# A 4096 x 4096 layer of a feed-forward stack by seven products of quarters instead of eight, and the stack in three token passes instead of two

## The reference, cut to what matters

```python
xn = layernorm(x)                                  # x: 4 x 4096 x 1024
out = x + attention(xn) + ffn(xn)                  # 16 heads of 64, ALiBi bias
def ffn(x):                                        # weights are -1, 0, 1, each with a scale per output row
    h = silu(tlin(x, w1)) * tlin(x, w2)            # 1024 -> 4096
    h = gelu(tlin(h, h1))                          # 4096 -> 4096
    h = gelu(tlin(h, h2))                          # 4096 -> 4096
    return tlin(h, w3)                             # 4096 -> 1024
# tlin(x, w) = (x @ w.T) * s
```

## Time and profile before

| | |
|---|---|
| median of 3 runs | 3135.11 us (3134.59 to 3135.47) |
| profiled execution | 3135.08 us; span 3133.5 us on core 5 (the cores' spans: 3117.3 to 3133.5) |
| TensorE busy | 3071.9 us, 98% of the span, 14592 matmuls |
| VectorE / ScalarE / GpSimd busy | 557.1 / 920.4 / 150.5 us |
| the tail (L677) | 9216 matmuls, from 1127.3 us to the end |
| granted TensorE clock | 0.995 on core 5, 0.997 to 0.998 on the others |

### The profile page before, as it was taken

How to read it: one execution, slowest core, us unless ns; L and a number is a source line. 1 busy time by engine, 2 the same in 40 slices (tenths; PEclk the granted TensorE clock), 3 DMA queues, 4 the chain that set the end, 5 groups by cost and what they waited for, 6 DMA issues and landing times.

```text
span 3133.5 us, 37072 instructions; the slowest of 8 cores (3117.3 to 3133.5 us)
## 1 busy us (share of the span) xinstructions
PE 3071.9 (98%) x14592; PEld 1341.0 (43%) x14592; DVE 557.1 (18%) x871; ACT 920.4 (29%) x1420; POOL 150.5 (5%) x252
## 2 busy tenths in 40 slices
PE   5999999999999999999999999999999999999999
PEld 3543333333333344444444444444444444444444
DVE  4523454444545420000000000011000000000001
ACT  3538778777777710000000000000000000000000
POOL 1210000000000000000000000000000000000000
PEclk9999999999999999999999999999999999999999
DMA  7414332333334663443444444587444443443453
GB/s 169 122 28 80 61 70 68 63 66 65 69 80 90 142 160 71 81 78 71 81 74 75 81 75 74 123 201 164 76 81 74 75 81 71 77 81 72 76 105 117
DMA packets 80279, 279.32 MB, mean 89 GB/s; under 512 B 8304, under 2 KB 28912, under 8 KB 59632
## 3 DMA queue, kind: packets, MB, share of 16 engines
q0 software_dynamic: 36192, 192.95, 35.5%
q1 hardware_dynamic: 42768, 81.91, 8.2%
q10 hardware_dynamic: 1152, 2.10, 0.2%
HBM read 436.31 MB, written 33.55 MB: 150 GB/s over the span
## 4 chain that ended last, share of the span: by engine, by line
PE 91%; DMA 7%; DVE 1%; issue 0%; ACT 0%; SPq 0%; POOL 0%; DVEq 0%; ACTq 0%; POOLq 0%
PE PS L677 59%; PE PS L169 21%; PE PS L585 7%; PE PS L561 4%; DMA out<-UO 4%; DMA Wv<-Wv 1%; DMA xin<-xk 1%; DMA h_d<-HO 1%; PE PS L307 0%; DMA XO<-xT 0%; SPq L69 0%; DVE st L282 0%; DVE st L283 0%; DVE UO L706 0%; DVE xnb L296 0%
## 5 line engine op out<-in xcount | busy, mean ns | idle before, releaser
L677 PE MATMUL PS<-HBb,WB 128*128 128x512 bf16 x4608 | 998.0, 380 | 7.0 <-DVE UO L706 4.3
L677 PE MATMUL PS<-HBa,WB 128*128 128x512 bf16 x4608 | 995.0, 379 | 3.8 <-ACT HBa L691 2.7
L677 PEld LDWEIGHTS PS<-HBb,WB 128*128 128x128 bf16 x4608 | 451.3, 98 | 553.5 <-issue 12.1
L677 PEld LDWEIGHTS PS<-HBa,WB 128*128 128x128 bf16 x4608 | 450.7, 98 | 548.2 <-issue 5.2
L573 ACT ACTIVATE eT<-PS,p 128x512 bf16<-128x512 f32 x972 | 591.4, 691 | 93.6 <-PE PS L561 93.6
L169 PE MATMUL PS<-XN,W 128*128 128x512 bf16 x2048 | 565.0, 381 | 4.8 <-DVE HO L456 3.9
L706 DVE SCALAR_TENSOR_TENSOR UO<-PS,cv,UO 128x512 f32<-128x512 f32 x32 | 24.0, 751 | 1833.9 <-PE PS L677 1832.6
L691 ACT ACTIVATE HBa<-PS,cv 128x1024 bf16<-128x1024 f32 x64 | 71.3, 1114 | 933.6 <-PE PS L677 933.6
L691 ACT ACTIVATE HBb<-PS,cv 128x1024 bf16<-128x1024 f32 x64 | 71.3, 1114 | 799.9 <-PE PS L677 799.9
L169 PEld LDWEIGHTS PS<-XN,W 128*128 128x128 bf16 x2048 | 180.3, 98 | 280.1 <-issue 97.5
L585 PE MATMUL PS<-eT,V 128*128 128x512 bf16 x972 | 296.9, 380 | 0.0
(11 more groups left out here) (52 smaller groups left out, 750.8 us busy)
## 6 DMA issues: line engine op xcount, KB each, us to landing
WB<-h1sl POOLq DMA_DIRECT2D x64, 1024.0 KB, 8.9
WB<-h2sl POOLq DMA_DIRECT2D x64, 1024.0 KB, 8.8
W<-w POOLq DMA_DIRECT2D x64, 512.0 KB, 6.1
xin<-xk SPq DMA_DIRECT2D x32, 512.0 KB, 5.1
h_d<-HO SPq DMA_DIRECT2D x128, 128.0 KB, 5.2
WB<-w3sl POOLq DMA_DIRECT2D x16, 1024.0 KB, 9.1
HBa<-h_d SPq DMA_DIRECT2D x8, 1024.0 KB, 7.4
UO<-acc_d SPq DMA_DIRECT2D x32, 256.0 KB, 3.4
```

The source lines that it names most:

```text
L677: f = lambda e, o=o, W=W, c=c, n=n, src=src: e.matmul(o, W[:, c, :], src[:, c, n * 512:(n + 1) * 512], start=(c == 0), stop=(c == 31))
```

## The change

The tokens go in three passes of 684, 684 and 680 (`HN` is half a pass: 342, 342, 340). h1 and w3 are computed as before, with matmuls over `HN` tokens, two per weight tile. h2 is cut in quarters: output rows in halves (slab j is paired with slab j + 16), inputs in halves (the first and last 16 tiles of a slab), and tokens in halves. Each pair of slabs then gives four output tiles, rows by tokens, by Winograd's form of Strassen's scheme: seven products of 16 matmuls instead of eight.

- h1's Gelu is written in f32 (`G`); for each pair of its slabs DVE forms four differences and ACT casts five tiles, which gives the seven right-hand sides `h11, h21, h22, t1, t2, t3, t4` in bf16 (`A`).
- For each pair of h2's slabs DVE forms four weight sums s1 to s4 (integers from -4 to 4, exact in bf16), each in two pieces of 1024 columns, in eight buffers `BS`. `pieces` places them between the instructions of the products: five pieces of pair j + 1 in pair j, and three of pair j after its first product.
- The seven products go to seven banks in turn; ACT copies the first (`p1`), DVE joins them in seven operations (`comb`), and four Gelus on ACT write h2's output to `HQ`.
- Weight buffers: three that stay (`C0` to `C2`), with two more in h1 (`E0`, `E1`, inside `HQ`), one more in h2 (`F0`, inside `HP`) and two more in w3 (`G0`, `G1`, inside `A`). `uses` lists the loads in order; `feed` issues the next ones when their buffer is free and its stage's gate is open. In h2 both buffers of a pair come free together, after the pair's third product and its last piece.
- w3 waits for the last Gelu only ahead of its tiles 15 and 31, which come last. The loads of `UO` and `XO` and the stores of the result go through ACT; `load_h` stays on SP.
- A tile `HO` that crosses the edge of a pass is stored by two DMAs (64 stores more).

The core of the diff:

```diff
+HN = [342, 342, 340]
+TOK = [0, 684, 1368]
+A_SZ = 16 * 342 * 2
+P0_AT = 65792
+P1_AT = P0_AT + 4 * A_SZ
+C_AT = P1_AT + 4 * A_SZ
...
+    h_d = nc.dram_tensor("h_d", [3, 128, 32, 684], BF16, kind="Internal").ap()
+    acc_d = nc.dram_tensor("acc_d", [8, 128, QC], F32, kind="Internal").ap()
...
-    HB = [sb("HBa", [128, 32, 1024], BF16, 65536), sb("HBb", [128, 32, 1024], BF16, 0)]
-    WB = [sb(f"WB{i}", [128, 32, 128], BF16, 131072 + 8192 * i if i < 2 else Q_AT + 8192 * (i - 2))
-          for i in range(6)]
-    UO = [sb(f"UO{i}", [128, 512], F32, DYN_AT + 4096 * i) for i in range(3)]
-    XO = [sb(f"XO{i}", [128, 512], F32, DYN_AT + 4096 * i + 2048) for i in range(3)]
+    A = {k: sb("A" + k, [128, 16, 342], BF16, A_SZ * i if i < 6 else DYN_AT + 11008)
+         for i, k in enumerate(("h11", "h21", "h22", "t1", "t2", "t3", "t4"))}
+    HP = sb("HP", [128, 32, 684], BF16, P0_AT)
+    HQ = sb("HQ", [128, 32, 684], BF16, P1_AT)
+    SLOT = {n: sb("W" + n, [128, 32, 128], BF16, at) for n, at in (
+        ("C0", C_AT), ("C1", C_AT + 8192), ("C2", C_AT + 16384), ("E0", 131072), ("E1", 139264),
+        ("F0", P0_AT), ("G0", 0), ("G1", 8192))}
+    BS = [sb(f"BS{i}", [128, 16, 128], BF16, at) for i, at in enumerate(
+        [DYN_AT + 11008 + A_SZ, C_AT + 24576] + [P0_AT + 8192 + 4096 * i for i in range(6)])]
+    G = [[sb(f"G{k}{i}", [128, 2, 342], F32, DYN_AT + 2752 * (2 * k + i)) for i in range(2)] for k in range(2)]
+    TF = [[sb(f"TF{k}{i}", [128, 342], F32, P1_AT + 1376 * (2 * k + i)) for i in range(2)] for k in range(2)]
+    R = {k: sb("R" + k, [128, 342], F32, DYN_AT + 1376 * i)
+         for i, k in enumerate(("p1", "u2", "u3", "c11", "c12", "c21", "c22"))}
+    UO = [sb(f"UO{i}", [128, 2, 342], F32, 16384 + 5504 * i) for i in range(3)]
+    XO = [sb(f"XO{i}", [128, 2, 342], F32, 16384 + 5504 * i + 2752) for i in range(3)]
...
-                    SP.dma(l_ho[u % 3], h_d[T][:, hid, tl * 512:(tl + 1) * 512], ho[:, :])
+                    for p in range(3):
+                        a, b = max(tc * 512, TOK[p]), min(tc * 512 + 512, TOK[p] + 2 * HN[p])
+                        if a < b:
+                            SP.dma(l_ho[u % 3], h_d[p][:, hid, a - TOK[p]:b - TOK[p]],
+                                   ho[:, a - tc * 512:b - tc * 512])
...
-            POOL.dma(l_wb[s % 6], WB[s % 6][:, :, :], (h1sl, h2sl, w3sl)[stg][i])
-
-    def load_h(T, chunks, *toks):
+            load_use(0, (PE.sem, PE.n))
+            load_use(1)
...
+    uses, use_of = [], {}
+    c = ["C0", "C1", "C2"]
+    for p in range(3):
+        for stg, ring, n in ((0, c + ["E0", "E1"], 32), (1, [c[2], c[0], c[1], "F0"], 32),
+                             (2, [c[2], c[0], c[1], "G0", "G1"], 8)):
+            for k in range(n):
+                use_of[p, stg, k] = len(uses)
+                uses.append((p, stg, k // 2 + 16 * (k % 2) if stg < 2 else k, ring[k % len(ring)]))
+        c = [c[2], c[0], c[1]]
+    use_tok = {}
+    def load_use(u, *toks):
+        _, stg, i, slot = uses[u]
+        POOL.wait(*toks)
+        use_tok[u] = POOL.dma(l_s[slot], SLOT[slot][:, :, :], (h1sl, h2sl, w3sl)[stg][i])
+    def load_h(p, chunks, *toks):
         SP.wait(*toks)
-        SP.wait(*t_hstore[T])
+        SP.wait(*t_hstore[min(p, 1)])
         for c in chunks:
-            SP.dma(l_hb[c], HB[T][:, 4 * c:4 * c + 4, :], h_d[T][:, 4 * c:4 * c + 4, :])
+            SP.dma(l_hb[c], HP[:, 4 * c:4 * c + 4, 0:2 * HN[p]], h_d[p][:, 4 * c:4 * c + 4, 0:2 * HN[p]])
...
-                load_h(0, [0, 1], (PE.sem, PE.n))
-                for s in range(2):
-                    load_wb(s, (PE.sem, PE.n))
+                load_h(0, [0, 1, 2], (PE.sem, PE.n))
+                load_use(3, (PE.sem, PE.n))
+                load_use(4)
             if qc == 3 and P == 4:
-                load_h(0, [2, 7], (PE.sem, PE.n))
+                load_h(0, [3, 4], (PE.sem, PE.n))
...
+    slot_free = {n: () if n[0] != "E" and n[0] != "C" else None for n in SLOT}
+    gate = {("C", p): () for p in range(3)}
+    n_use = [5]
+    def feed():
+        while n_use[0] < len(uses):
+            p, _, _, slot = uses[n_use[0]]
+            if slot_free[slot] is None or (slot[0], p) not in gate:
+                break
+            load_use(n_use[0], *slot_free[slot], *gate[slot[0], p])
+            slot_free[slot] = None
+            n_use[0] += 1
+    def done(u, *toks):
+        slot_free[uses[u][3]] = toks
+        feed()
...
+        for j in range(16):
+            t_gl = []
+            for hf in range(2):
+                u = use_of[p, 0, 2 * j + hf]
+                W = SLOT[uses[u][3]]
+                pp = n_p[0] % 4
+                n_p[0] += 1
+                PE.wait(use_tok[u], bank_free[2 * pp], bank_free[2 * pp + 1])
+                for t in range(2):
+                    o = BK[2 * pp + t][:, 0:n]
+                    for c in range(32):
+                        if j == 0 and hf == 0 and t == 0 and c % 4 == 0:
+                            PE.wait(l_hb[c // 4].tok())
+                        f = lambda e, o=o, W=W, c=c, t=t, n=n: e.matmul(
+                            o, W[:, c, :], HP[:, c, t * n:(t + 1) * n], start=(c == 0), stop=(c == 31))
+                        if c == 31:
+                            tok = PE.do(f)
+                        else:
+                            PE.raw(f)
+                done(u, tok)
+                g = G[j % 2][hf]
+                ACT.wait(tok, *t_sum.get(j - 2, ()), *t_tmp)
+                c0 = 80 + j + 16 * hf
+                t_gl.append(ACT.do(lambda e, g=g, pp=pp, c0=c0, n=n: e.activation(
+                    g[:, :, 0:n], halves(pp, n), AF.Gelu, bias=0.0, scale=cv[:, c0:c0 + 1])))
+                bank_free[2 * pp] = bank_free[2 * pp + 1] = t_gl[-1]
...
+            DVE.wait(*t_gl, *t_last, *t_sum.get(j - 2, ()))
+            ACT.wait(*t_gl, *t_last)
+            d3 = diff(t3, h22, ALU.subtract, h12)
+            diff(to("t1"), h12, ALU.subtract, h11)
+            d2 = diff(t2, t3, ALU.add, h11, d3)
+            for k, a in (("h11", h11), ("h21", h21), ("h22", h22)):
+                cast(k, a, None)
+            cast("t3", t3, d3)
+            t_sum[j] = (diff(to("t4"), t2, ALU.subtract, h21, d2), cast("t2", t2, d2))
+        t_h1 = (PE.sem, PE.n)
+        gate["F", p] = (t_h1,)
+        feed()
...
+        def sums(j):
+            w11, w12, w21, w22 = quarters(j)
+            for k in range(4):
+                bsum[j, k + 1] = [n_s[0] % 8, None, None]
+                n_s[0] += 1
+            s1, s2, s3, s4 = [BS[bsum[j, k][0]] for k in (1, 2, 3, 4)]
+            for k, a, op, b, dst, dep in ((1, w21, ALU.add, w22, s1, None), (2, s1, ALU.subtract, w11, s2, 1),
+                                          (3, w11, ALU.subtract, w21, s3, None), (4, w12, ALU.subtract, s2, s4, 2)):
+                slot = bsum[j, k][0]
+                for h in range(2):
+                    DVE.wait(use_tok[use_of[p, 1, 2 * j]], use_tok[use_of[p, 1, 2 * j + 1]], *bs_free[slot])
+                    if slot >= 2:
+                        DVE.wait(t_h1)
+                    if dep:
+                        DVE.wait(bsum[j, dep][1 + h])
+                    r = slice(8 * h, 8 * h + 8)
+                    bsum[j, k][1 + h] = DVE.do(lambda e, dst=dst, a=a, b=b, op=op, r=r: e.tensor_tensor(
+                        dst[:, r, :], a[:, r, :], b[:, r, :], op))
+                    yield
...
+        def prod(k, a, j):
+            b = n_b[0] % 8
+            n_b[0] += 1
+            slot, t0, t1 = bsum[j, k]
+            PE.wait(bank_free[b], t0, t1)
+            tok = part(b, BS[slot], a, range(16), True, True)
+            bs_free[slot] = (tok,)
+            return b, tok
...
+        cur = sums(0)
+        pieces(cur, 5)
+        for j in range(16):
+            u1, u2 = use_of[p, 1, 2 * j], use_of[p, 1, 2 * j + 1]
+            w11, w12, w21, w22 = quarters(j)
+            b1, b2, b4 = [(n_b[0] + i) % 8 for i in range(3)]
+            n_b[0] += 3
+            PE.wait(use_tok[u1], bank_free[b1], bank_free[b2])
+            if j == 0:
+                PE.wait(*t_sum[14])
+                part(b1, w11, "h11", range(15), True, False)
+                part(b2, w12, "h21", range(15), True, False)
+                PE.wait(*t_sum[15])
+                m1 = part(b1, w11, "h11", [15], False, True)
+                m2 = part(b2, w12, "h21", [15], False, True)
+            else:
+                m1 = part(b1, w11, "h11", range(16), True, True)
+                m2 = part(b2, w12, "h21", range(16), True, True)
+            ACT.wait(m1, *fr["p1"])
+            p1 = bank_free[b1] = ACT.do(lambda e, n=n, b1=b1: e.copy(R["p1"][:, 0:n], BK[b1][:, 0:n]))
+            pieces(cur, 1)
+            PE.wait(use_tok[u2], bank_free[b4])
+            m4 = part(b4, w22, "t4", range(16), True, True)
+            pieces(cur, 1)
+            c11 = bank_free[b2] = comb("c11", "p1", b2, ALU.add, m2, p1)
+            gelu("c11", 0, 0, j, c11)
+            pieces(cur, 1)
```

(98 more changed lines are left out.)

102 lines of the change are left out of this document (46 added, 56 removed).

## The result

The changed kernel took 3118.85 us (median of 7 runs) beside 3135.93 us before; by ratio it stands at 0.9942 of before, 95% interval 0.9931 to 0.9954: 18 us gained, not 103, and outside the stated range.

What follows compares the result with a forecast made beforehand. TensorE was taken to bound the kernel, by number of matmuls times spacing. From 3135.08 us, -100.6 for matmuls, -2.7 for waits and +0.5 at the end made -102.8: 3032.3 us, range 3022 to 3072.

Steps and rivals of the forecast that it cites:

- The spacing at 342 columns: Tail matmuls: a line through three traced sizes gives 145.0 ns at 342 columns and 144.1 at 340.
- The sum on TensorE: h1, h2 and w3: 13056 matmuls make 1889.2 us against 1989.8 before, 100.6 less.
- VectorE in h2: DVE's pieces and joins in h2: 9.0 to 16.3 us a pair, hidden behind TensorE's 16.24; rival that DVE bounds h2, 0.07.
- Weights in h2: Slab loads in h2: 129 GB/s needed, DMA share 0.72, in time by 3 us for DVE and 10 for TensorE.
- The edges from h1 to h2: ACT's and DVE's work between h1 and h2 mostly hides behind matmuls; 1 us an edge, 3 in all.
- the mechanism I had named as a rival: Matmuls of 342 columns dearer because rows of 684 bytes start at new places; 7.9 ns each cancels the gain; chance 0.04.
- In the first two w3 stages: Edges at w3, where h chunks, two slabs and UO and XO tiles start together: 2 us each, between 0 and 10.
- The edges of w3 cost more: Rival: 10 us at each of two w3 edges and 4 at each from h1 to h2, +25, 3057 us; chance 0.07.
- It now goes by ACT's queue: At w3's edges, the result's store no longer waits behind h loads on SP's queue, which cost 4.3 us once before.
- The end: After the last matmul: a join over 680 columns for 512 and a 340 KB store for 256, together +0.5 us.
- Ahead of the tail: Before 1127 us only 64 extra stores are new, beside attention: 0 us, between -1 and +5.
- the 9.8 that the forecast allowed for waits and the clock: Tail: 3 us for h1-to-h2 edges, 4 for the first two w3 stages, 2.8 for the clock; 12.5 before.

Runs made afterwards that it cites:

- x4_prod8: Changed kernel with one of the seven products of each pair computed twice, so h2 has eight products again: 1.0307 of the kernel before, 3236 us.
- x10_axpool: Changed kernel with x added during attention (its loads on POOL), 344-element rows, eight UO buffers, banks emptied by ACT, w3's loads and stores on SP: 3064.7 and 3062.8 us.
- x3_pad344: Changed kernel with the rows of the seven right-hand sides 344 elements apart instead of 342: 0.9907 of the kernel before.
- x2_store_sp: Changed kernel with the stores of the result back on SP's queue, behind the eight loads of h: 0.9872 of the kernel before.
- x1_acc8: Changed kernel with eight UO and XO buffers instead of three, all loads issued at a w3 stage's start: 0.9887 of the kernel before.
- x5_h_late: Changed kernel with the eight loads of h issued two at a time after w3's second to fifth slab: 0.9940 of the kernel before.
- x6_evac: Changed kernel with 344-element rows, five buffers, w3's banks copied to SBUF by ACT, loads and stores on SP: 3104.1 and 3102.6 us.
- x7_no_h: Changed kernel without the second and third pass's h loads, DVE writing zeros instead (output wrong): 0.9780 of the kernel before, 3070 us.
- x8_fold: Changed kernel with x added during attention instead of in w3, so the XO loads leave the tail: 0.9871 of the kernel before.

## Why the prediction was wrong

Right, by its own steps:
- *The spacing at 342 columns*: 297.15 us for 2048 against 297.0. The Trainium skill ("TensorE: Matmul & The Clock Gate", "Back-to-back issue gap") has a sustained stream at about 81 ns for 128 columns and 131 for 512. These traces don't agree with either: 56 and 215.9 ns. The 11 ns more at 342 columns that the prediction held against itself came from the first of these alone.
- *The sum on TensorE*: x4_prod8 gives the removed product back for 115 us, and x10_axpool's core 1 has the whole tail at the forecast length.
- *VectorE in h2*: a piece of 1024 bf16 columns takes 685 ns, the lower end of the bounds; 512 columns in f32 took 687. The Trainium skill, "VectorE: DVE Perf Modes", section "The perf-mode tier table (the rule you actually need)", gives a bf16 tensor_tensor in SBUF twice the f32 rate, and the trace agrees. DVE is busy 133.7 of 263 us, 8.4 us a pair of slabs, less than the 9.0 to 16.3 allowed.
- *Weights in h2*: share 0.71 and 133 GB/s, forecast 0.72 and 129; no wait of TensorE for a slab. (That all eight cores had drawn more at once is not in the earlier trace rows, which show core 5 alone; in 2022 to 2125 us of the kernel before they moved 178 to 206 GB/s.)
- *The edges from h1 to h2*: no idle time; I had allowed 3 us.

Off in size: h2's matmuls took 146.9 ns instead of 145.0 because of the rows of 684 bytes, +9.0 us (x3_pad344). It is the mechanism I had named as a rival, at a quarter of the price it needed.

Failed: *"In the first two w3 stages ... I take 2 us for each, between 0 and 10."* They cost 35.0 and 31.5. So the step that failed is this term, 2 us where some 33 came, taken over from a reading of the kernel before in which a store behind the h loads was the cost. I had put the DMA rate of the earlier trace rows against h2's need, but never summed w3's. In its 74.2 us fall eight slabs (8.4 MB), h (5.6), the UO and XO tiles (5.6) and the stores (2.8): 22.4 MB, which would be 302 GB/s. The best average in the rows was 238, and 183 to 207 came [the windows above]. The rival "The edges of w3 cost more" named the right place, but took 10 us an edge, a third of what came.

Nor is one rate enough, since the queues differ. By the shares of the first edge shown above, 6.39 MB of weights took 38 us of all 16 engines (5.9 us a MB), h's 5.60 MB 17.8 us (3.2) and 3.50 MB of tiles and stores 12.8 us (3.7). As an estimate from these, the whole stage's bytes need 50 + 18 + 31 = 98 us of full engines in a stage of 74. The same view of the kernel before, in 2014 to 2125 us (here q1, SP's, has h, the tiles and the stores):

```profile
q0 software_dynamic: 1152, 8.39, 42.6%
q1 hardware_dynamic: 4368, 14.26, 40.7%
```

There a MB of weights took 5.6 us and of the rest 3.2, and the stage's 29.4 MB need 114 us by it, in a stage of 110.7: hardly too much. What was over (22.7 MB moved in the stage) went into the next h1, while the banks held for 55 us, and TensorE waited only 4.3 us. The change took a quarter off the bytes and a third off the time, raised the steady draw of the weights from 76 to 109 GB/s in h1, shortened the banks' cover to 37 us and made two such edges of one. The prediction has the steady draw, the cover and the number of edges; it lacks the sum.

The Trainium skill, "HBM Reference", section "Specifications (TRN2)", gives each of two cores that share an HBM domain about 358 GB/s. As an estimate from that page, the stage's traffic counted at HBM (slabs as f32, 8.4 MB more) is 30.8 MB, 86 us for a stage of 74. The trace shows 15.55 MB in 75 us there, 21.9 MB counted that way (the weights' 6.39 MB twice), 292 GB/s: less than the page's figure, with the DMA engines 0.92 busy.

Also failed, with its sign: *"It now goes by ACT's queue"* as a relief. x2_store_sp undid it and gained 22 us.

*The end*: +0.5 forecast, +11 measured (14.5 against 3.5). Through three buffers the load for the last tile waits for a store, and the last two are summed and stored after the last matmul; with eight buffers it was 5.2 (x1_acc8).

*Ahead of the tail*: 1130.0 us against 1127.3, +2.7, within what I gave; the cores of two runs of the same kernel differ by more (1121 to 1133).

The terms: 2.7 (start of the tail) + 0.2 (h1's matmuls) + 9.0 (h2's) + 35.0 + 31.5 (the two edges) + 10.5 (the end, beyond the forecast's 0.5) = 88.9. Less the 9.8 that the forecast allowed for waits and the clock, that is 79.1; the miss was 3110.9 - 3032.3 = 78.6.

Of the prediction's own signs, TensorE idle under 15 us in the whole tail did not come (49.6); the signs that it gave for being wrong, h2 over 270 us or h1 over 146 ns, did not come either. They watched h2, and the loss was in w3.

Open: why one order at the edges is 20 us better than another at equal bytes (x2_store_sp, x1_acc8, x5_h_late), and what the two cores of a pair share, and why the first one gets more of it.

## What to carry to other kernels

When a stage is made shorter, sum the bytes that fall into each of its stretches, with their due times, against the rate the trace has shown, above all where the mean share is low: 0.7 in h2 was no problem and 0.6 in h1 neither, yet the two w3 stages of 74 us between them ate two thirds of the forecast gain (66.5 of 102.8 us). Sum the time of the DMA engines and not only bytes, since a MB of one queue can take nearly twice that of another. A wait for bytes moved when its cover or its order was changed (x1_acc8, x5_h_late, x6_evac) and shrank when the bytes went (x7_no_h, x8_fold). And price an idle stretch of TensorE with the half-clock matmuls behind it: here nearly a third more on top.

## What the runs showed of the hardware that was not expected

- A DMA issue can hold its engine long. In x1_acc8 the sixteen loads at the start of a stage were issued by ACT; from the tenth on an issue took up to 16 us instead of 0.5 (start us, us):

```profile
1697.75 0.69 ACTq L75 DMA_DIRECT2D UO<-acc_d  x1
1698.46 15.98 ACTq L75 DMA_DIRECT2D XO<-xT  x1
```

- With moving rows (the matmul's right-hand side) packed 684 bytes apart a matmul took 146.9 ns on average, with rows 688 apart 145.0 (x3_pad344).
- Of two neighbouring cores, the one that began w3 11 us earlier moved 239 GB/s in it and the other 222, and the later one lost 28 us more at the edges (x10_axpool, cores 1 and 0).
- A MB of weights, cast from f32 on the way, took 5.9 us of all 16 DMA engines; a MB of h 3.2 (first edge of the changed kernel).
